# A Mamba-style block beside a gated feed-forward layer: the five engine programs written out for all sixteen blocks instead of looping

## What is computed

```
xn  = (x - mean) / sqrt(var + 1e-5)
# branch 1, a state-space layer
z, xs, B, C, dt = split(xn @ in_proj_w)            # 1024, 1024, 64, 64, 16 columns
v   = silu(causal_conv(xs, 4 taps) + bias)         # 16 heads of 64
k,q = elu(B) + 1, elu(C) + 1
a   = exp(-softplus(dt + dt_bias) * exp(A_log))
y   = scan over time with decay a (in chunks)  + D * v
y   = y * rsqrt(mean(y*y) + 1e-6) * norm_scale * silu(z)
out1 = y @ out_proj_w
# branch 2, a gated feed-forward layer with Hadamard transforms
h    = fwht(xn * SU_ug)/64;  h = silu(h @ W_gate.T * s1) * (h @ W_up.T * s2)
out2 = (fwht(h * SU_dp)/64) @ W_down.T * s3
out  = x + out1 + out2
```

## Time and profile before

| | |
|---|---|
| median of 3 runs | 1883.05 us (1882.88 to 1883.23) |
| the profiled execution, span from first to last instruction | 1883.3 us |
| preparation, from the span's start to PE's first matmul of block 0 | 163.5 us |
| blocks 0 to 15 on PE | 163.5 to 1877.0 us |
| tail (last loads, final sum, store) | 6.3 us |
| PE busy over the span | 1808.6 us, 96% |
| DVE, ACT, POOL busy | 1387.9, 1228.6, 308.9 us |
| mean granted TensorE clock | 0.991 of full speed |

### The profile page before, as it was taken

The page is one execution under the profiler, slowest core; times in us unless marked ns, Lnnn a source line. Parts: engine busy times, 40 slices in busy tenths (PEclk is TensorE's granted clock), DMA queues, the critical chain, the costliest instruction groups (busy, mean ns, idle before and its releaser), DMA issues.

```text
span 1883.3 us, 40159 instructions
## 1 busy us (share of the span) xinstructions
PE 1808.6 (96%) x13745; PEld 1244.5 (66%) x13746; DVE 1387.9 (74%) x2859; ACT 1228.6 (65%) x2583; POOL 308.9 (16%) x270
## 2 busy tenths in 40 slices
PE   5779999999999999999999999999999999999998
PEld 2346767576776767576766768677675757666674
DVE  6986867768585877758585877858686786848686
ACT  7957848476665848566574848556583857658483
POOL 0000202112030202103030211203020211203020
PEclk9989999999999999999999999999999999999999
DMA  8212122221312222121312222121312312131222
GB/s 320 71 65 57 47 57 80 46 71 34 79 43 75 62 57 79 32 71 44 81 46 58 79 46 74 37 72 46 88 49 57 79 32 82 34 80 46 61 75 57
DMA packets 217544, 125.60 MB, mean 67 GB/s; under 512 B 179662, under 2 KB 180790, under 8 KB 216886
## 3 DMA queue, kind: packets, MB, share of 16 engines
q1 hardware_dynamic: 216870, 122.30, 24.0%
q10 hardware_dynamic: 528, 1.05, 0.2%
HBM read 72.18 MB, written 8.65 MB: 43 GB/s over the span
## 4 chain that ended last, share of the span: by engine, by line
PE 80%; DVE 10%; issue 3%; DVEq 2%; SPq 2%; ACT 1%; DMA 1%; ACTq 0%
PE bank L912 78%; SPq L873 1%; DVE pair L228 1%; DVE pair L230 1%; DVEq L1287 1%; DVE wi L666 1%; DVEq L1312 1%; DVE v L1289 1%; DVE Mx L1271 1%; DVE wug L624 1%; PE bank L728 0%; PE bank L732 0%; DMA wi<-n_L_attn_out_proj_w_dram 0%; PE bank L729 0%; DVE pair L223 0%
## 5 line engine op out<-in xcount | busy, mean ns | idle before, releaser
L912 PE MATMUL bank<-pair,wug 128*128 128x256 f16 x6144 | 699.8, 273 | 0.0
L912 PEld LDWEIGHTS bank<-pair,wug 128*128 128x128 f16 x6144 | 596.3, 98 | 90.3 <-issue 3.4
L912 PE MATMUL bank<-wd,h 128*128 128x512 f16 x1536 | 360.4, 379 | 1.8 <-DVE h L1244 1.6
L1186 POOL TENSOR_TENSOR state<-state,dec 128x512 f32<-128x512 f32 x64 | 80.0, 1260 | 1104.1 <-ACT neg L1101 830.7
L1233 DVE SCALAR_TENSOR_TENSOR pair<-pair,conv 128x256 f32<-128x256 f32 x384 | 180.1, 513 | 105.5 <-ACT pair L1049 94.8
L912 PEld LDWEIGHTS bank<-wd,h 128*128 128x128 f16 x1536 | 148.0, 98 | 165.4 <-DVE h L1244 5.1
L912 PE MATMUL bank<-wi,pair 128*128 128x512 f16 (+1 forms) x1152 | 200.3, 328 | 3.6 <-DVEq L1346 3.0
L912 PE MATMUL bank<-pair,wi 128*128 128x256 f16 x1536 | 183.8, 282 | 18.9 <-issue 18.9
L912 PEld LDWEIGHTS bank<-pair,wi 128*128 128x128 f16 x1536 | 154.7, 101 | 41.9 <-issue 20.1
L1115 ACT ACTIVATE Mx<-Mx,cs_own 128x128 f32<-128x128 f32 x512 | 162.2, 387 | 6.3 <-DMA Mx<-cs_rows 5.9
L912 PEld LDWEIGHTS bank<-wi,pair 128*128 128x128 f16 x1152 | 99.6, 98 | 100.0 <-DVEq L1346 3.8
(11 more groups left out here) (253 smaller groups left out, 2716.0 us busy)
## 6 DMA issues: line engine op xcount, KB each, us to landing
Mx<-cs_rows SPq DMA_DIRECT2D x128, 256.0 KB, 3.6
pair<-in_L_attn_u_dram SPq DMA_DIRECT2D x17, 512.0 KB, 3.3
Mx<-in_L_attn_u_dram SPq DMA_DIRECT2D x16, 512.0 KB, 3.6
out_dram<-Mx SPq DMA_DIRECT2D x16, 512.0 KB, 2.8
big<-in_L_ffn_W_down_dram SPq DMA_DIRECT2D x2, 2048.0 KB, 16.8
wug<-in_L_attn_in_proj_w_dram SPq DMA_DIRECT2D x2, 2048.0 KB, 12.6
pair<-in_L_ffn_W_gate_dram SPq DMA_DIRECT2D x4, 1024.0 KB, 5.3
pair<-in_L_ffn_W_up_dram SPq DMA_DIRECT2D x3, 1024.0 KB, 15.5
```

The source lines that it names most:

```text
L912: ins = nc.tensor.matmul(out, lhsT, rhs, start=first and n == 0, stop=last and n == len(pairs) - 1)
L1186: pool.tensor_tensor(half, half, bcast(dec3[:, 2, c, 8 * hf:8 * hf + 8], HD), ALU.mult).then_inc(state_faded, 1)
```

## The change

Every loop is replaced by a Python loop that records `body` once for each of the 16 block numbers. The steps, their order, the buffers and the semaphores stay as they are; the values of the waits become constants, and the register instructions that computed them and the branches go. `start_sequence()` is still called once before block 0 and once before block 8.

```diff
@@ sync
             body(0, 1, first=True)
-            with sp.Fori(0, NBLOCKS - 2) as f:
-                body(f + 1, f + 2)
-            body(NBLOCKS - 1, 0)
+            for i in range(1, NBLOCKS):
+                body(i, (i + 1) % NBLOCKS)
@@ tensor
-            with pe.Fori(0, NBLOCKS // 2) as j:
-                body(j * 2)
-                body(j * 2 + 1)
+            for i in range(NBLOCKS):
+                body(i)
@@ scalar
-            with act.Fori(0, NBLOCKS) as j:
-                body(j)
+            for i in range(NBLOCKS):
+                body(i)
@@ gpsimd
-            with pool.Fori(0, NBLOCKS) as i:
+            for i in range(NBLOCKS):
@@ vector
-            body(0, first=True)
-            with dve.Fori(0, NBLK - 1) as j:
-                body(j + 1)
-            start_sequence()
-            with dve.Fori(0, NBLK) as j:
-                body(j + NBLK)
+            for i in range(NBLOCKS):
+                if i == NBLK:
+                    start_sequence()
+                body(i, first=i == 0)
```

## The result

The kernel before ran in 1883.14 us (median of 4 runs, 1882.88 to 1885.22), the changed one in 1848.42 us (4 runs, 1847.27 to 1850.79). The ratio is 0.9825, 95% interval 0.9807 to 0.9843, so 1.6 to 1.9% faster.

What follows compares the result with a forecast made beforehand. PE was taken to bound the kernel, busy 1808.6 of 1883.3 us. 1883.3 - 28.45 (PE's jumps) + 1.9 (waits returning) - 1.2 (register instructions) = 1855.6 us, range 1848.5 to 1863.

Steps and rivals of the forecast that it cites:

- The pause belongs to PE's jump back: Even blocks from 2 on, behind `bc`: PE's seven jumps cost 18.9 us of pause and 9.55 us of low clock.
- the net 26.5 of the forecast: Even blocks 2 to 14: 28.45 us of pause and low clock gone, 1.9 us back as waits for h and x.
- The rival that it belongs to the code's place whether or not there is a jump: Pause behind `bc`: due to the code's place or a fetch straight code makes too; time stays 1883 us; chance 0.04.
- The 18.9 us of "issue": PE after 165 us: seven idle gaps for which the profile shows no awaited cause, 18.9 us in all, expected to go.
- No lag builds up: Block starts: DVE waits about 5.8 us for `bc` each time, so odd blocks are a fair model for all.
- Other engines' code costs nothing: All blocks: some 55 more code packets for the other engines cost nothing; upwards 0.4 us per block, 6 us, kept.
- The slower rival: Chain making h's low half: DVE's code fetch stalls 3.5 us in each of 15 blocks, giving 1909 us; chance 0.04.
- the one of new waits: All 15 blocks: without the pause PE waits 1 us more for h or x, giving 1872 us; chance 0.12.
- the step on the register instructions: PE's waits for h or x: removing register instructions saves 1.2 us, about a quarter of 4.4 us.
- that of PE's jumps: Even blocks: removing PE's seven jumps saves 28.45 us, 18.9 of pause and 9.55 of low clock.
- all blocks as short as block 0: All 16 blocks last 104.9 us like block 0, giving 1848 us, more gain than forecast; chance 0.08.
- the signs that I had named for being right: New profile: no PE "issue" row, blocks 105.0 to 105.9 us, clock never under 1.00, some 55 more packets, fewer instructions.

## Why the prediction was right, and where it was short

*The pause belongs to PE's jump back.* Right. It vanished with the loop (29.6 us less in blocks 1 to 15 with PE alone written out, against the net 26.5 of the forecast), came back with it, and moved and vanished with the place of the loop's head. The rival that it belongs to the code's place whether or not there is a jump is excluded, and with it, as a price for PE's jumps, the about 108 ns that the Trainium skill (Advanced Engine Details and Errata, Control Flow Timing) gives a compare-and-branch. ACT and DVE took about half of that, 45 and 56 ns, and PE's jump 3540 at the median.

*Its parts.* The 18.9 us of "issue" were taken as one quantity. They were two: about 1.2 us per jump for a fetch that starts too late, and 1.5 us for the 512 KB load ahead of it on the DMA engines. In the one execution with that load moved no low clock followed the pauses either. This changed no number of the forecast, but I had not seen the cheaper remedies.

*No lag builds up.* Right: DVE waits for `bc` 5.5 us per block in the changed kernel too (87.8 us in 16).

*Other engines' code costs nothing.* Right. The queue moved 74 packets, 57 more than the 17 of the kernel before, against 55 forecast. DVE shows a few gaps by "issue" of up to 0.5 us, some 4 us together in blocks 1 to 15, and PE waits for none of them. The slower rival did not happen, and neither did the one of new waits.

*What failed* is the step on the register instructions: "Of those waits I take about a quarter, 1.2 us", out of a bound of 15 x 0.29 = 4.4 us. They were worth 5.4 us, more than the bound. The bound was read from PE's idle time, 0.29 us per odd block, but an idle time in these rows starts only where the recorded duration of the matmul before it ends, and that reaches past the point where its successor could have started (379 ns recorded at a pace of 216 for 512 columns). The wait for h in block 3 is listed as 0.40 us and delays PE by 0.57. A safe bound stood one group further up: 105.47 - 104.9 for block 0, 0.57 us per block, 8.5 in 15, of which the waits for h are only a part. The reason I gave for the quarter, that the chain goes through data instructions more than through the sequencer, overlooked the repeated 0.2 us gaps behind the drains. I had also counted DVE's register instructions at one line, 15 per block; the changed kernel has 812 fewer on DVE's sequencer and engine together, some 50 per block. DVE reached the low half of h 0.9 us earlier in block 1, where PE had lost 0.6 by waiting for it, so the whole wait went.

*A second term was too small*, that of PE's jumps. The forecast has 28.45 less 1.9, 26.5 net; 29.6 were measured. The idle times understate here too. By lengths, pause and clock made 29.9 us of the even blocks, and the late first matmul behind the jump, which I had taken for a wait on the transposes of x that stays, another 1.4 of the odd ones, all but 0.3 of which went with the loop; about 1.7 us came back as waits for h in the unpaused even blocks.

In numbers: for blocks 1 to 15 the forecast was 26.5 + 1.2 = 27.7 us, measured 29.6 + 5.4 = 35.0. Of the missing 7.3, 3.1 belong to PE's jumps and 4.2 to the register instructions. Both errors have the same sign, so nothing cancelled, and the result came within 0.1 us of the range only because the case "all blocks as short as block 0", 1848 us and a chance of 0.08, had set it. That case is what happened. Of the signs that I had named for being right, the blocks' length, 105.0 to 105.9 us, was missed at 104.9.

## What to carry to other kernels

When a loop's body on the engine that bounds the kernel is longer than what stays on the chip, look behind the loop's first matmuls for a gap by "issue": here it stood where the head's portion of code ends and was longer with a 512 KB load issued just before the jump. Moving that load took away half of each pause, and moving the loop's head all of it, as writing the loop out does. Writing out a second engine can pay if the first waits for it and its chain has drains followed by waits on computed values. Here PE and DVE were enough, and the other three could stay loops. To bound what a wait is worth, compare lengths of equal blocks, not idle times.

## What was not expected of the hardware

- A PE loop of some 1730 instructions is fetched again in every pass, while the loops of ACT and DVE, 278 and 288 instructions per block, caused no packet on their queue in blocks 2 to 7.
- Behind PE's jump the next portion's packet starts 0.7 to 0.9 us after the branch where the 512 KB load was issued 3 us or more before the branch's end (15 jumps of the loop over one block), and 2.5 to 2.6 us after it where the load was issued 0.7 us before.
- The clock fell behind 6 of 7 pauses of 2.5 to 2.9 us in the profile before and behind 4 of 7 of 1.9 to 2.5 us in one experiment, and never behind the pauses of up to 2.1 us in three others. Before block 0 it fell behind waits of 2.99 and 3.01 us (the loop over one block, the load moved) and not behind others of 3.0 us (the kernel before; the changed one with PE's loop over two blocks): a pause's price in clock varies from one execution to the next, by 1.5 us each.
- Two waits on semaphores in a row share one instruction: 64 more waits made 32 more instructions in the profile, and 160 made 80 (38221 against 38141).
